# Where the eight factors of the last layer are summed: from the context stage to the differential-attention stage

## The reference

```python
# layer 1, attention: 16 heads, difference of two score matrices inside one softmax
lam = exp(dot(lambda_q1, lambda_k1)) - exp(dot(lambda_q2, lambda_k2)) + LAMBDA_INIT
score = softmax(attn1 - lam * attn2, axis=-1)
x = x + ((1 - LAMBDA_INIT) * einsum('bhts,bshd->bthd', score, v)) @ W_proj

# layer 1, last block: factors is (8, 512, 512)
mixed = einsum('btd,rde->bte', layernorm(x), factors)
x = x + mixed / sqrt(8) + bias
```

## Time and profile before

| | |
|---|---|
| median of 3 runs | 2528.97 us (2526.53 to 2531.1) |
| profiled execution: its own time | 2532.93 us |
| span of its trace | 2531.1 us |
| mean granted TensorE clock | 0.936 of full |
| busy share: PE, DVE, POOL, ACT | 86%, 70%, 43%, 37% |
| context stage | about 930 to 1216 us |
| differential-attention stage | about 1818 to 2410 us |

### The profile page before, as it was taken

The page is one execution under the profiler, slowest core; times in us unless marked ns, Lnnn a source line. Parts: engine busy times, 40 slices in busy tenths (PEclk is TensorE's granted clock), DMA queues, the critical chain, the costliest instruction groups (busy, mean ns, idle before and its releaser), DMA issues. The chain is left out here.

```text
span 2531.1 us, 25434 instructions
## 1 busy us (share of the span) xinstructions
PE 2178.9 (86%) x7344; PEld 1121.6 (44%) x7344; DVE 1774.3 (70%) x2992; ACT 932.2 (37%) x1772; POOL 1083.8 (43%) x805
## 2 busy tenths in 40 slices
PE   6998998999899967675489898999589999999848
PEld 2544544555455533332355555555233333334234
DVE  1887688778768867777488988988636464554454
ACT  1443333343333324333364645556113232232310
POOL 2454333335434314545589898999500000000033
PEclk9999999999999988877699999999779999999879
DMA  6000000000000031334853645443222122221021
GB/s 250 18 22 18 17 21 21 21 17 17 21 18 22 22 108 69 142 143 161 304 172 123 205 141 191 170 161 143 71 79 62 40 50 50 50 50 38 13 103 51
DMA packets 95550, 214.80 MB, mean 85 GB/s; under 512 B 15824, under 2 KB 33104, under 8 KB 93024
## 3 DMA queue, kind: packets, MB, share of 16 engines
q1 hardware_dynamic: 77184, 156.18, 18.9%
q10 hardware_dynamic: 17760, 57.42, 6.5%
q0 software_dynamic: 512, 0.13, 0.0%
HBM read 146.30 MB, written 42.07 MB: 74 GB/s over the span
## 5 line engine op out<-in xcount | busy, mean ns | idle before, releaser
L706 POOL TENSOR_SCALAR a_prob<-a_prob,a_rsum 128x256 f32<-128x256 f32 x256 | 147.1, 593 | 466.2 <-DVE a_rsum L634 466.0
L1342 DVE TENSOR_TENSOR_SCAN s_state<-s_decay,s_state 128x512 f32<-128x512 f32 x256 | 305.0, 1212 | 12.8 <-ACT s_decay L1284 12.5
L1298 POOL TENSOR_TENSOR s_state<-s_b_rows,s_delta_u 128x1024 f32<-128x1024 f32 x128 | 303.4, 2382 | 16.8 <-DMA s_b_rows<-scan_bc 14.4
L1460 PE MATMUL c_bank<-c_xn_parts,c_w_parts 128*128 128x512 f32 (+1 forms) x1056 | 271.9, 408 | 1.5 <-DVE c_xn_parts L1536 1.4
L1284 ACT ACTIVATE s_decay<-s_delta,s_a 128x512 f32<-128x512 f32 x256 | 173.6, 690 | 220.3 <-DVE s_state L1342 219.7
L2006 POOL DMA_DIRECT2D d_qs<-d_neg_t x16 | 8.2, 514 | 515.5 <-DVE d_neg_t L1937 515.5
L438 PE MATMUL a_bank<-a_xn_t,a_wq 128*128 128x512 f32 x512 | 227.2, 592 | 0.0
L1460 PEld LDWEIGHTS c_bank<-c_xn_parts,c_w_parts 128*128 128x128 f32 (+1 forms) x1056 | 197.8, 188 | 62.3 <-issue 14.2
L521 PE MATMUL a_bank<-a_wo,a_out_t 128*128 128x512 f32 x512 | 222.3, 592 | 0.0
L549 ACT ACTIVATE a_prob<-a_score,a_neg_m 128x256 f32<-128x256 f32 x256 | 117.9, 475 | 275.5 <-DVE a_neg_m L629 275.3
L1858 ACT ACTIVATE d_prob_t<-d_score 128x512 f32<-128x512 f32 x256 | 139.0, 595 | 194.5 <-PE d_score L1741 193.5
(11 more groups left out here) (197 smaller groups left out, 3764.5 us busy)
## 6 DMA issues: line engine op xcount, KB each, us to landing
s_b_rows<-scan_bc SPq DMA_DIRECT2D x64, 512.0 KB, 3.8
c_w_parts<-ffn_weights_hi ACTq DMA_DIRECT2D x39, 512.0 KB, 3.7
c_w_parts<-ffn_weights_lo ACTq DMA_DIRECT2D x39, 512.0 KB, 4.6
f_idx<-in_idx SPq DMA_DIRECT2D x64, 130.0 KB, 2.1
ffn_weights<-f_picks SPq DMA_DIRECT2D x64, 130.0 KB, 1.8
r_factor<-in_factors SPq DMA_DIRECT2D x8, 1024.0 KB, 8.1
d_qs<-d_hi SPq DMA_DIRECT2D x128, 64.0 KB, 2.0
d_ks<-d_hi SPq DMA_DIRECT2D x128, 64.0 KB, 2.0
```

The lines of the kernel that those rows point to most:

```text
L1298: pool.tensor_tensor(self.state[:, s], row.broadcast_to([P, 2, T]), self.delta_u[:, h % 2], ALU.mult) \
L1342: dve.tensor_tensor_scan(self.state[:, s, e, :], self.decay[u % 2][:], self.state[:, s, e, :], 0.0, ALU.mult, ALU.add).then_inc(self.scann ...
L1460: mm = nc.tensor.matmul(banks[b][0:width[o], :], w_parts[:, n % SLOTS, w, at:at + width[o]], xn_parts[:, x_, k, :], start=((k, w, x_) == t ...
```

## The change

The tiles, loads, adds and the store leave the context stage. In the differential-attention stage each group n = 4i + g handles rows g*128 to g*128+127 of two factors: SP issues one load of 512 KB behind `stack`, and GpSimd makes two adds of 128x512 at the head of its group, ahead of `store_maxima`. The sum lies in the tile `lam_v`, free once the two dot products of lambda are done. The sum is stored after the last pass.

```diff
@@ stage_context
-    factor = sb("r_factor", [P, 2, KD, D], F32)
-    factor_sum = sb("r_factor_sum", [P, KD, D], F32)
...
             with sp.Fori(0, B) as i:
-                for s in range(2):
-                    sp.wait_ge(factor_added, i * PER_PASS + max(s, 1))
-                    sp.dma_start(factor[:, s], dram["factors"][i * PER_PASS + s]
-                                 .rearrange("(k p) e -> p k e", p=P)).then_inc(factor_in[s], 16)
                 split.load(sp, i, 0)
...
-            sp.wait_ge(factor_added, RANK + 1)
-            sp.dma_start(scratch["factor_sum"], factor_sum[:]).then_inc(stored, 16)
-            sp.wait_ge(stored, B * STORES + 16 + 1)
+            sp.wait_ge(stored, B * STORES + 1)
...
-                for s in range(2):
-                    pool.wait_ge(factor_in[s], i * 16 + 16)
-                    pool.wait_ge(factor_added, i * PER_PASS + s + 1)
-                    nc.gpsimd.tensor_tensor(factor_sum[:], factor_sum[:], factor[:, s], ALU.add) \
-                        .then_inc(factor_added, 1)
                 split.subtract(pool, i, 0)
...
-            nc.gpsimd.memset(factor_sum[:], 0.0).then_inc(factor_added, 1)
@@ stage_diff_attention
+    factor = sb("d_factor", [P, 2, PER_PASS, D], F32)
+    factor_sum = lam_v
...
+            def load_factors(i, g):
+                s = g % 2
+                sp.wait_ge(factor_added, (i * GROUPS + g) * PER_PASS + 1 - (PER_PASS if g else 0))
+                sp.dma_start(factor[:, s], dram["factors"][bass.ds(i * PER_PASS, PER_PASS), g * P:(g + 1) * P, :]
+                             .rearrange("r p e -> p r e")).then_inc(factor_in[s], 16)
+
             def one_pass(i, more):
                 for g in range(GROUPS):
                     if more or g + 2 < GROUPS:
                         stack(ring, i, (g + 2) % GROUPS)
+                    load_factors(i, g)
...
             passes(sp, one_pass)
+            sp.wait_ge(factor_added, RANK * KD + 1)
+            sp.dma_start(scratch["factor_sum"], factor_sum[:]).then_inc(factor_stored, 16)
+            sp.wait_ge(factor_stored, 16)
...
+            def add_factors(i, g):
+                s = g % 2
+                pool.wait_ge(factor_in[s], (i * (GROUPS // 2) + g // 2) * 16 + 16)
+                for r in range(PER_PASS):
+                    pool.wait_ge(factor_added, (i * GROUPS + g) * PER_PASS + r + 1)
+                    nc.gpsimd.tensor_tensor(factor_sum[:, g, :], factor_sum[:, g, :], factor[:, s, r, :], ALU.add) \
+                        .then_inc(factor_added, 1)
+
             def one_pass(i, more):
                 for g in range(GROUPS):
+                    add_factors(i, g)
                     if more or g + 1 < GROUPS:
                         store_maxima(ring, i, (g + 1) % GROUPS)
...
             store_maxima(first, 0, 0)
+            pool.wait_ge(lam_step, 3)
+            nc.gpsimd.memset(factor_sum[:], 0.0).then_inc(factor_added, 1)
             passes(pool, one_pass)
```

More of the change, by code:

```diff
@@ L1615, in stage_diff_attention @@
     out_t = sb("d_out_t", [P, GROUPS, T], F32)
+    PER_PASS = RANK // B
+    assert PER_PASS == 2 and GROUPS == KD
+    factor = sb("d_factor", [P, 2, PER_PASS, D], F32)
+    factor_sum = lam_v
+    factor_in = core.sems("d_factor_in", 2)
+    factor_added = core.sem("d_factor_added")
+    factor_stored = core.sem("d_factor_stored")
     banks = [psum(f"d_bank{b}", [P, 512], F32) for b in range(4)]
```

## The result

The change makes the kernel slower: 2588.18 us (median of 4, 2586.62 to 2589.15) against 2530.03 us, a ratio of 1.0229 with a 95% interval of 1.0215 to 1.0243. The forecast was 2588 us. The span of the trace went from 2531.1 to 2586.3 us.

The account below looks back on a forecast made before the run. It took chains of waits as the bound: VectorE's convolution in the context stage, TensorE's queue in attention. Stalls 79 plus half clock 21 less context gain 41 made 59 us on 2528.97, so 2588 us, range 2560 to 2616.

Parts of the forecast that it names:

- The chain of the stall: Differential attention: maxima store waits for adds, adds for a load behind the copies; 9.1 us from copies to TensorE, 7.4 stall.
- The terms of 79 and 21 us: Differential attention: 79 us of TensorE stalls over all passes, plus 21 us of half-clock matmuls behind them.
- The clock term: TensorE at half clock after idling: attention loses 11 x 1.9 = 21 us; context saves 1.7 us four times, 6.8 us.
- The two queue orders: Differential attention: SP's load stands behind the group's 24 copies, GpSimd's adds ahead of the next store of maxima.
- The context gain: Context stage: 25.5 + 6.9 + 6.8 + 2 = 41 us gained by removing adds, loads and store; bounds 32 and 46.
- 8.5 + 1.7: Context passes 1 to 3: 8.5 us each from VectorE instructions no longer held, 1.7 us from `dbl` at full clock.
- Pass 0: Context stage, first pass: two held VectorE instructions freed, 6.9 us, plus 1.7 us of TensorE's clock.
- the end: Context stage end: without the last store of the sum, about 2 us of landing before the barrier saved.
- the one in which the clock does not matter: Rival, attention stalls: TensorE's slow start is absorbed because ScalarE partly paces its groups; 2567 us, chance 0.12.
- The slow load: Rival, attention: load lands in 5.8 us and adds take 1.66, 36 us more over 14 stalls; 2624 us, chance 0.07.
- The hidden adds: Rival, attention: factors are in before `neg_t` is ready, leaving only the context saving; 2488 us, chance 0.05.
- the missing context gain: Rival, context stage: VectorE's hold moves to the subtractions, so nothing is saved there; 2629 us, chance 0.03.

Follow-up runs that it names:

- e10: Changed kernel with TensorE kept busy in the stalls by repeated score matmuls, 26 ahead of groups 1 and 3, 20 ahead of group 2 (26 in last pass): 2568.3 us.
- e1: Changed kernel with SyncE issuing each group's factor load ahead of that group's 24 copies: 2493.59 us.
- e2: Changed kernel with loads still late, but GpSimd sending the maxima and computing rstd before it waits for the factors and adds: 2491.15 us.
- e4: Changed kernel with GpSimd still waiting for the factors ahead of the store of maxima, but adding only after it and rstd: 2561.09 us.
- e8: Changed kernel with two adds of 128x2048 put back into each context pass, on a tile of zeros without any load: 2627.06 us.
- e3: Changed kernel with the sum left out altogether, no factor loads or adds in either stage, a tile of zeros stored instead: 2493.45 us.

## Why the prediction was right

The mechanisms were right. That the total was met to 0.2 us is luck: attention lost 92.5 us where 79 + 21 = 100 were forecast, the context stage gained 43 where 41 were, and the feed-forward stage lost 6 where nothing was. The two traces lie 55 us apart and the medians 58, where 59 were forecast.

- **The chain of the stall** was as argued: the store of maxima behind the adds, the adds behind a load, the load behind the copies. The load landed in 3.7 us, not 4.0, and from the last copy to TensorE it took 8.4 us in group 4, not 9.1. With that group 3 does not stall at all (0.9 us were expected) and the 11 others are on average 0.4 us shorter. The last of them was longer, 8.6 us: in the last pass SyncE issues three loads within 7 us, and the store of maxima beside them took 3.5 us to land, not 1.7. First `columns` were 35.5 to 37.2 us apart, not 34 to 36. The terms of 79 and 21 us measured 72 (92.5 less the clock's part) and 20.8 us.
- **The clock term** was right at 1.9 us a time; e10 takes just this out. Left out, the forecast would have missed by 21 us.
- **The two queue orders** are each sufficient: turning one round removes the whole loss (e1, e2). e4 shows the adds as 27 us of it.
- **The context gain** came out at 43 and not 41 us. From one `dbl` to the next, passes 1 and 2 gave 10.6 and 10.4 us (8.5 + 1.7 forecast) and pass 3 gave 12.9, of which 1.7 us lies in 16 matmul records that take 7.1 us now and took 8.8, partly at half clock, before. Pass 0 gave 6.7 us (8.6 forecast) and the end 2.8 (2 forecast). Two steps were wrong. The clock term came in three passes and not in four: in pass 0 TensorE still waits 5.58 us for Silu, and `dbl` takes 5.79 us there, against 5.33 before. And in passes 1 to 3 the subtractions no longer cost VectorE anything. ScalarE rounds at 1018.8, 5.6 us after the first tap, and VectorE is through at 1021.7. The taps gained 11.3 us, not 8.5, but `dbl` then had to wait for TensorE's own four preceding products, which run at half clock, so part of it was not cashed.
- **Not foreseen**: the feed-forward stage, +6 us, which made up for most of attention's lower loss. Without it the result would have been 2582 us.

That VectorE's instructions with two SBUF inputs stand still during GpSimd's adds in SBUF is shown by e8: 19.73 us for twelve taps that take 8.46 alone. The Trainium skill (SBUF — State Buffer, section Who interferes with whom) states that a VectorE instruction with two SBUF inputs contends with a GpSimd instruction that reads SBUF. The 5.00 us of a 0.73 us instruction and the 19.73 us above agree with it. What decides which of the two is held, VectorE as in pass 0 or GpSimd as in pass 1, no run here isolates.

Of the rivals, e10 decides against the one in which the clock does not matter. The slow load did not come: 3.4 to 5.1 us from issue to landing over the 16 loads, 3.7 in the median, and adds of 1.26 us. The hidden adds are what e1 and e2 make true, and the missing context gain is ruled out by the stage's 242.8 us and by e3.

## What to carry to other kernels

Idle time of an engine is not slack. Look at what it waits for: if each wait ends in something that must go out at once, new work belongs behind that, or its inputs must be in well before; here 30 us of idle time per group held 2.2 us of slack, and moving one line is worth 3.7% (2588 to 2491 us). A stall of TensorE costs its length plus the slow restart behind it. And where a freed stage seems to be bound by one engine, price adds and transfers apart: here either alone would have kept a part of the cost, 42 or 17 us.

## What was not expected of the hardware

- A stage with the same instructions took 607.3, 610.7 and 613.6 us, with 61, 71 and 78 us of it at half clock. Such a difference needs no difference in the kernel: the first two are profiles of one kernel.
- Matmuls of 96x512 in a row took 0.245 us each. An idle stretch of 2.6 us behind 3.9 us of them was still followed by half clock (0.70 granted over the next 5.6 us).
- Either party can be held: beside free-running taps a subtraction on GpSimd took 3.50 us and the next, behind them, 1.65; before, where VectorE was held, the two took 4.12 us.
